# The square of a feed-forward block's middle layer: from a ScalarE activation to a GpSimd product, in a kernel ordered by a planner

## The reference

```python
x = x + 0.5 * ffn(layernorm(x))
x = x + attn(layernorm(x))        # 16 heads of 16, rotary embedding, causal softmax, biases
x = x + 0.5 * ffn(layernorm(x))

def ffn(x):                        # mu_r, mu_k: one number per channel
    x_prev = x shifted by one token, zero in front
    xr = mu_r * x + (1 - mu_r) * x_prev
    xk = mu_k * x + (1 - mu_k) * x_prev
    r = sigmoid(xr @ W_r.T)
    k_act = square(relu(xk @ W_k.T))
    return r * (k_act @ W_v.T)
```

## Time and profile before

| | us |
|---|---|
| median of 3 runs (lowest, highest) | 3132.23 (3127.75, 3134.32) |
| the profiled execution's own time | 3136.11 |
| its span, first to last instruction | 3134.3 |
| PE busy | 2978.4 |
| DVE busy | 2512.8 |
| ACT busy | 2158.8 |
| POOL busy | 1566.8 |

### The profile page before, as it was taken

How to read it: one execution, slowest core, us unless ns; L and a number is a source line. 1 busy time by engine, 2 the same in 40 slices (tenths; PEclk the granted TensorE clock), 3 DMA queues, 4 the chain that set the end, 5 groups by cost and what they waited for, 6 DMA issues and landing times.

```text
span 3134.3 us, 57243 instructions
## 1 busy us (share of the span) xinstructions
PE 2978.4 (95%) x18245; PEld 1669.6 (53%) x18245; DVE 2512.8 (80%) x8326; ACT 2158.8 (69%) x4802; POOL 1566.8 (50%) x2190
## 2 busy tenths in 40 slices
PE   6799999999999999999999999999999999999987
PEld 5444555555555555555555555555555555555434
DVE  3788888888888888888888888888888888888862
ACT  4477777777777777777777777777777776777664
POOL 5454545455454455455555455455555555454322
PEclk9799999999999999999999999999999999999998
DMA  3433442443433352343443434343343443343411
GB/s 97 80 70 65 77 94 63 92 86 68 88 80 85 73 96 67 76 100 61 88 90 70 87 77 88 68 97 72 69 100 67 83 89 75 84 76 80 76 45 38
DMA packets 202593, 245.55 MB, mean 78 GB/s; under 512 B 68406, under 2 KB 104246, under 8 KB 202294
## 3 DMA queue, kind: packets, MB, share of 16 engines
q1 hardware_dynamic: 202293, 241.90, 37.2%
HBM read 53.48 MB, written 51.38 MB: 33 GB/s over the span
## 4 chain that ended last, share of the span: by engine, by line
PE 68%; DVE 14%; ACT 8%; POOL 4%; issue 4%; SPq 1%; DMA 1%; POOLq 0%; DVEq 0%; ACTq 0%
PE ps_y L720 15%; PE ps_s L689 13%; PE ps_m L699 11%; DVE ps_m L926 7%; PE ps_d L779 7%; PE ps_d L773 6%; PE ps_d L785 5%; PE ps_d L776 5%; ACT pt_sb L815 4%; PE ps_d L766 3%; PE ps_d L727 2%; PE ps_d L789 2%; DVE dif_sb L956 2%; DVE sw_sb L979 1%; DVE ka_sb L950 1%
## 5 line engine op out<-in xcount | busy, mean ns | idle before, releaser
L815 ACT ACTIVATE pt_sb<-ps_s 128x512 f32<-128x512 f32 (+3 forms) x3072 | 1465.0, 494 | 844.7 <-PE ps_s L689 834.6
L926 DVE CUSTOM_DVE_ANT_0 ps_m<-ps_m,mask_sb 128x512 f32<-128x512 f32 (+3 forms) x3072 | 1676.1, 570 | 447.7 <-PE ps_m L699 430.4
L689 PE MATMUL ps_s<-qr_sb,kr_sb 99*128 99x512 bf16 (+3 forms) x3072 | 1009.3, 331 | 54.3 <-ACT pt_sb L815 42.3
L699 PE MATMUL ps_m<-kr_sb,qr_sb 96*128 96x512 bf16 (+3 forms) x3072 | 1001.3, 329 | 45.2 <-DVE mx_sb L926 40.7
L1057 POOL TENSOR_SCALAR_AFFINE_SELECT pt_sb<-pt_sb 128x512 f32<-128x512 f32 x512 | 331.1, 647 | 850.3 <-ACT pt_sb L815 849.3
L720 PE MATMUL ps_y<-pt_sb,v_sb 128*32 128x512 f32 (+3 forms) x6144 | 595.2, 498 | 1.2 <-POOL pt_sb L1057 1.2
L689 PEld LDWEIGHTS ps_s<-qr_sb,kr_sb 99*128 99x128 bf16 x3072 | 294.8, 96 | 528.4 <-issue 234.6
L699 PEld LDWEIGHTS ps_m<-kr_sb,qr_sb 96*128 96x128 bf16 x3072 | 302.3, 98 | 329.2 <-DVE mx_sb L926 99.6
L926 DVE DVE_READ_ACCUMULATOR2_ANT mx_sb<- 128x1 f32 x3072 | 431.2, 140 | 0.0
L785 PE MATMUL ps_d<-axn_sb,wqk_sb 128*128 128x256 f32 x1024 | 307.7, 399 | 4.0 <-ACT axn_sb L857 3.9
L720 PEld LDWEIGHTS ps_y<-pt_sb,v_sb 128*32 128x32 f32 x6144 | 155.1, 109 | 284.8 <-issue 261.5
(11 more groups left out here) (92 smaller groups left out, 3277.8 us busy)
## 6 DMA issues: line engine op xcount, KB each, us to landing
kr_sb<-part_sb SPq DMA_DIRECT2D x378, 128.0 KB, 4.4
qr_sb<-part_sb SPq DMA_DIRECT2D x378, 128.0 KB, 4.7
y_way<-yt_sb SPq DMA_DIRECT2D x128, 256.0 KB, 2.6
sw_sb<-qb_sb SPq DMA_DIRECT2D x496, 64.0 KB, 2.0
x_sb<-x SPq DMA_DIRECT2D x64, 256.0 KB, 2.8
yn_sb<-y_way SPq DMA_DIRECT2D x64, 256.0 KB
den_sb<-r_way SPq DMA_DIRECT2D x64, 256.0 KB
out<-x_sb SPq DMA_DIRECT2D x64, 256.0 KB, 2.2
```

What stands on the lines that cost most here:

```text
L689: eng.matmul(ps_s[:, slot % NS, 0:width], kr_sb[0:KR + NP, n % RS, j, kb * P:(kb + 1) * P], qr_sb[0:KR + NP, n % RS, j, q0:q0 + width], st ...
L699: eng.matmul(ps_m[:, u % NM, 0:width], qr_sb[0:KR, n % RS, j, i * P:(i + 1) * P], kr_sb[0:KR, n % RS, j, piece * QC:piece * QC + width], s ...
L815: eng.activation(pt_sb[:, buffer, j, column:column + width], ps_s[:, slot % NS, 0:width], ACT.Exp, scale=SCALE).then_inc(exped, 1)
L926: eng.tensor_tensor_reduce(ps_m[:, u % NM, 0:width], ps_m[:, u % NM, 0:width], mask_sb[:, m0:m0 + width], 1.0, -3e38, ALU.add, ALU.max, mx ...
```

## The change

The square is taken from ACT and made by POOL, as a product of `ka_sb` with itself in place. In the plan its cost is 1.2 (POOL) in place of 0.55 (ACT), it stands two slots behind the ReLU rather than zero, and `f_V` three slots behind it rather than two. PE waits for the same semaphore, `f_square`.

```diff
             s("ACT", "f_relu", p, 0.5, t, ("f_K", p, 1))
-            s("ACT", "f_sq", p, 0.55, t, ("f_relu", p, 0))
+            s("POOL", "f_sq", p, 1.2, t, ("f_relu", p, 2))
             s("PE", "f_R", p, 4, t, ("f_K", p, 0), ("f_r1", p, 3))
             s("ACT", "f_tanh", p, 0.47, t, ("f_R", p, 1))
-            s("PE", "f_V", p, 4, t, ("f_R", p, 0), ("f_sq", p, 2))
+            s("PE", "f_V", p, 4, t, ("f_R", p, 0), ("f_sq", p, 3))
...
-                elif name == "f_sq":
-                    act.wait_ge(*taken_from("f_K", i))
-                    eng.activation(ka_sb[:, i % 2, :, :], ka_sb[:, i % 2, :, :], ACT.Square).then_inc(f_square, 1)
...
+                elif name == "f_sq":
+                    pool.wait_ge(*taken_from("f_K", i))
+                    eng.tensor_tensor(ka_sb[:, i % 2, :, :], ka_sb[:, i % 2, :, :], ka_sb[:, i % 2, :, :], ALU.mult).then_inc(f_square, 1)
```

## The result

| | before | after |
|---|---|---|
| median, us (lowest to highest, 5 executions each) | 3134.28 (3127.75 to 3138.3) | 3149.99 (3145.19 to 3152.78) |
| span of the profiled execution, us | 3134.3 | 3148.2 |

The ratio is 1.0055, with a 95% interval of 1.0041 to 1.0068: the changed kernel is slower by 13 to 21 us. The prediction had 3124 us, with 3107 to 3143 for 8 in 10; its likeliest case was faster, and its range does not hold the result. Of all executions behind this document one, of the kernel with the product in four pieces, took 3747.71 us at a granted clock of 0.75, where the others had 0.98 to 0.99; it is left out.

What follows compares the result with a forecast made beforehand. The prediction took the kernel to be bound by TensorE's list in order, with small holes. Its terms, -18 + 4 + 5 + 1 = -8 us, gave 3124 us, with 3107 to 3143 for 8 in 10.

Steps and rivals of the forecast that it cites:

- VectorE is held by GpSimd: VectorE's operations with two SBUF inputs are held while GpSimd works; 12 us more hold, +5 us, bounds 0 and +10.
- the rotary step behind it: `r_cos` right behind a product is late by up to 1.16 us, but VectorE's `r_add` has time to spare: 0.
- The relief, -18: ScalarE loses 128 squares, so TensorE waits less for it: -18 us, bounds 0 and -40.
- The selects and `f_V`, +4: Selects delayed behind GpSimd's product, +1 us, and `f_V` waiting for it in tight chunks: +4 us together, bounds 0 and +25.
- the product is late for `f_V`: Rival: GpSimd still busy when the ReLU lands, so `f_V` waits in 47 chunks; 3149 us, chance 0.20.
- The lock in full, 3178: Rival: every product holds a VectorE operation for its 1.16 us, 59 us reaching TensorE; 3178 us, chance 0.03.
- Start and end, +1 and 0: Products ahead of attention statistics and `r_QK` at the start, +1 us, bounds 0 and +3; last `f_V` not delayed, 0.

Runs made afterwards that it cites:

- writes of 180 us: Kernel before, squares still on ScalarE, with eight memsets of 128x100 added on GpSimd at the place of the product: 3143.75 us, 1.0038.
- the four memsets of 90 us: Kernel before, squares still on ScalarE, with four memsets of 128x100 added on GpSimd beside every square from the fifth chunk on: 3132.21 us, 0.9992.
- the swap with `r_cos`: Changed kernel with `r_cos` put ahead of the product on GpSimd wherever the two stood in adjacent slots: 3147.81 us, 1.0049.

## Why the prediction was wrong

**The step that failed** is "VectorE is held by GpSimd", +5. It was made of two factors, and both were low. The hold was taken at 0.084 us for each us that GpSimd works, from an average over its operations outside the selects: 12 us. On an equal plan it is 2573.0 - 2534.8 = 38 us, or 38 / 143.5 = 0.27 for each us of product. The share that reaches TensorE was taken at 0.4, from the visible waits over the reckoned holds; between the same two kernels it is 26 / 38 = 0.7. Together 26 us in place of 5, outside the bound of 10.

The first factor has two causes. Counted in the traces as above, GpSimd's work outside the selects held VectorE for (107 - 22) / 1236 = 0.07 of its time in the kernel before, and the new products do so for 20 / 143.5 = 0.14 of theirs: they stand where more of VectorE's steps start. And "the rotary step behind it", put at 0, was not 0: the prediction asked whether `r_add` would be late, not whom `r_cos` holds when it runs later itself, and under `r_cos` and `y_mul` another 22 us came. (The prediction's own 0.084 counts the holds of the selects without their time, which made it a little high, not low.) Of VectorE's 60 us, the remaining 22 come with the new order, and cost nothing that shows in the time.

**The relief, -18.** Its sign was right, its size and its source were not. New plan without square and without product: 3121.68 against 3131.85, so -10 us. Of this the order brings 8 and the lighter engine 2. The wait fell below 30 as said, but as much with the squares on ScalarE. One reason for the small part of the engine: the squares' durations add up to 81.9 us, but ScalarE's busy time differs by only 2166.0 - 2105.6 = 60 us between the new plan with and without them, since neighbours overlap: in the kernel before the square starts 0.13 us before the end of what is ahead (median), and its own end is overlapped in turn. ScalarE's busy time after, 2106.0, was foretold as 2077 for the same cause and for exponentials that are busy for 1479.6 us in place of 1465.0.

**The selects and `f_V`, +4.** Small, as said: one wait of 1.5 us and none more for selects. The rival "the product is late for `f_V`" gave 3149 us, and the measured median is 3149.99; it is nevertheless wrong, since its waits are not there. A number that fits shows nothing when the row that it rests on is missing.

**The lock in full, 3178.** Its mechanism was the right one and its size was too large. A product holds only if a two-input operation of VectorE starts under it. It assumed 148 us of hold under the products where 20 came, 38 with all that they displaced, and a pass of 0.4 where 0.7 came. A chance of 0.03 was too little for a mechanism whose maxima were in the rows.

**Start and end, +1 and 0.** The start did not get longer. The first score product stands at 88.7 us, before at 90.8; six kernels with the plan of before, whose additions begin later than that, have it at 89.1 to 90.6 us, so most of these 2 us may be no more than what executions differ by. The +1 is not seen. In the first 160 us the kernel after has 511 matmuls recorded, against 476, at a granted clock of 0.91 against 0.84 in the earlier trace rows; the busy times of the two, 114.5 and 116.3 us, can't be compared at different clocks. At the second sequence's first score product the kernel after is 4 us ahead (303.9 against 308.1 us), at the last one 14 us behind (3102.0 against 3087.7), and from there to the end both take 46 us. So the whole loss, 18 us, lies in between, at full clock, where TensorE's busy time between 270 and 2900 us falls from 2555.9 us to the second of these lines:

```profile
0.00:160.00 160.00, 114.53 (x511) 73.07 (x511) 101.01 (x315) 66.10 (x131) 89.82 (x132) 0.91 0.38 87
270.00:2900.00 2630.00, 2545.07 (x15878) 1444.70 (x15871) 2235.29 (x7241) 1826.57 (x4068) 1479.89 (x2002) 1.00 0.38 80
```

**The sum by what was measured**: -10 for order and relief, +28 for the product in both its ways (hold and longer list), makes +18; the ratio of 1.0055 is +17. This only divides the difference at the kernel without a square, so it had to close; it does not test the parts.

**What stays open.** How much of the 28 us of time is the product's own hold and how much the displacement of GpSimd's other operations. Of what VectorE is held for, the two have about half each. In time, writes of 180 us put the displacement at 13 us and the four memsets of 90 us at none, but the displaced order differs each time, so that between a half and all of the 28 us is the hold itself is an estimate and not shown. Why the swap with `r_cos` freed 14 us of VectorE and no time is open too. And why the new order is faster by 8 us although VectorE is held for longer in it was not tried: it is a fact of the rows of the table, without a cause.

## What to carry to other kernels

Where VectorE feeds the bound engine, work moved to GpSimd is priced by its kind and by what it pushes back. A GpSimd product stopped each two-input operation of VectorE that started under it until its own end, and 128 of them at 1.1 us cost 24 to 28 us where VectorE had stood idle for 20% of the span; about half of the added hold came under products that were there before and now ran later. Take such a price from who meets whom in the new order, not from the mean excess over all of GpSimd's time. And where a change goes through a planner, run the new plan with the old placement too: here it is the better kernel, 3123.94 us.

## What the runs showed of the hardware

GpSimd's operation with one tensor and a constant takes 1506 ns for 128x512, longer than the product of two tensors at 1160 and of a tile with itself at 1065 to 1121 in the means. It let a two-input operation of VectorE through in 0.48 us with 0.91 us of its own left, and held only those that started in its first 0.4 us, where in the kernel after an operation with two tensors or a select, of 128x512, let none of 299 through that started under it with 0.25 us or more left. Cutting a product of 1.12 us in four gives pieces of 455 ns, 1.7 us together (217.2 / 128).
